# Warm-up of expert weights: the low halves of six experts computed on VectorE instead of GpSimd, and one GELU moved ahead

## The chip, the cores and the metric

The kernel runs on one core of a Trainium2 chip. The metric is the time of one execution on the device, in microseconds (us). Engines are named as the profile names them: PE is TensorE (PEld its weight loads), DVE is VectorE, ACT is ScalarE, POOL is GpSimd, SP is SyncE, which here issues all transfers.

## The reference

Sixteen batches of 256 tokens with 256 features pass through four sublayers, each with a residual. Layer norms stand in front.

```python
x = x + latent_cross_attention(ctx, layernorm(x))     # 8 heads of 128, keys from ctx and x: 512 of them
x = x + ffn_with_token_updates(layernorm(x))          # 256 -> 1024, exact GELU, -> 256
x = x + cross_attention(layernorm(x), ctx, ctx)       # one head of 256
x = x + experts(layernorm(x))                         # 8 experts, all computed, weighted by a router

# experts:
gate = einsum('btd,edi->beti', x, Wg)                 # (8, 256, 256) weights per expert
up = einsum('btd,edi->beti', x, Wu)
h = silu(gate) * up
out = einsum('bte,betd->btd', weights, einsum('beti,eid->betd', h, Wd))
```

## The kernel before, in words

**Three products for one.** Every operand of a large product is split into a high half (the value rounded to fp32r by a copy) and a low half (value minus high half). `product` issues three matmuls for each part: high by high, high by low, low by high. The high halves are made by ACT (names ending in `_high`), the low halves by DVE (`_low`), with a subtraction that has to follow its high. Expert weights are split once, in three pieces each (gate, up and down: `expert_piece`), and stay in memory.

**Two programs one behind the other.** `latent_attention` is the first sublayer: a loop over 16 batches with 8 heads, slots h = 0 to 7. In a slot PE computes the scores of head h + 1 into two `sim` banks, then works through an order of fills (K, Q, V projections, transposed probabilities T, outputs O) in a ring of four PSUM banks. A fill waits until the low half of the fill four places ahead of it has been taken out of the same bank (`ring_lo`). ACT takes the high half and computes the exponentials, DVE the low half and the maxima, POOL normalises the probabilities. `ffn_attention_experts` holds the other three sublayers. Its first batch is worked in beside the last batch of the first program, by hooks: `beside(h, done)` is called at named places in each engine's order of that batch. Where a hook stands in the order of its own engine decides what it is ahead of, since each engine works strictly through its own list.

**The turns.** After that, `rest()` runs turns t = 1 to 16. Turn t carries the chain of batch t (feed-forward, attention) and the experts of batch i = t - 1, interleaved: PE does gate e, up e, a piece of the chain, down e - 1. Between experts ACT does `silu` and `hidden_high`, DVE `hidden`, `hidden_low` and `weigh` (expert e's weighted sum), with the steps of the chain between. Turn 1 is written out by itself (`warm`): in it the weights of experts 2 to 7 are also split. PE's `split(e)` makes it wait for `warm_lo` to reach 3e + 3 ahead of gate e. Turns 2 to 14 are a hardware loop, 15 and 16 follow. All other turns have no splitting in them.

**The places that the change touches.** In turn 1, ACT does the highs of the experts at places that `WARM_AT` lists: expert 2 at the head of the turn, expert 3 between the second and the third GELU, experts 4 and 5 behind hidden_high 2, expert 6 behind the V copy, expert 7 behind hidden_high 4. POOL does all their lows (`expert_low`, L1042 to L1046), in the order 2, 3, 4, 5, then an rstd, 6, an rstd, 7. Experts 0 and 1 are split by ACT and DVE earlier. In the last batch of the first program, `gelu_high(0, 3)` and `gelu_low(0, 3)` stand behind K 4 of slot 2 on ACT and on DVE; h_fill(0, 3), which they read, stands behind K 4 on PE.

Of the kernel before, what the change touches and what calls it, by code (L numbers as in the profile page):

```python
# [9 lines left out]
ALU = mybir.AluOpType  # L10
# [11 lines left out]
def f32(ap):  # L22

    return ap.bitcast(F32)
# [723 lines left out]
def ffn_attention_experts(nc, ctx, mem, first, x1, ctxT, out, W1T, b1, W2T, b2, scale, WqT, bq, WkT, bk, WvT, bv, Wg, Wu,  # L748
# [9 lines left out]
    HC = HID // P  # L758
# [48 lines left out]
    Q, K, V, PT = 0, 2, 4, 6  # L807
# [97 lines left out]
    def expert_piece(e, j):  # L905
        return [w[e][:, j].rearrange("p c d -> p (c d)") for w in (we_raw, weh, wel)]

    WARM_AT = {2: 0, 3: 1, 4: 2, 5: 2, 6: 3, 7: 4}

    def warm_in(slot):  # L910

        return [e for e, s in WARM_AT.items() if s == slot]

# [90 lines left out]
    def gpsimd(pool):  # L1004
        def take(s, value):

            pool.wait_ge(s, value)
            pool.sem_inc(took, 1)

        def rstd_of(n, w):  # L1010
            take(var_ready[w], n + 1)
            nc.gpsimd.tensor_scalar(veps[:], mv[:, :, 1], EPS, 1.0, ALU.add, ALU.mult).then_inc(veps_ready[w], 1)
            pool.wait_ge(veps_ready[w], n + 1)
            nc.gpsimd.tensor_tensor(rstd[:], veps[:], mhalf[:], ALU.pow).then_inc(rstd_ready[w], 1)

        def bias_x1(n):

            pool.wait_ge(ln_ready["A"], n + 1)
            nc.gpsimd.tensor_tensor(x1_s[:], x1_s[:], b2_b[:].unsqueeze(1).to_broadcast([P, ST, D]), ALU.add)\
                .then_inc(x1_biased, 1)  # L1020

        def bias_x2(n):

            pool.wait_ge(ln_ready["B"], n + 1)
            nc.gpsimd.tensor_tensor(x2_s[:], x2_s[:], bv_b[:].unsqueeze(1).to_broadcast([P, ST, D]),
                                    ALU.add).then_inc(x2_biased, 1)

        def odd_rows(n):

            take(lo["A"], n + 1)  # L1030
            for part, xt in enumerate((xth, xtl)):
                nc.gpsimd.tensor_copy(
                    od[:, :, 0:8 * NL].rearrange("p c (i z h) -> p c i z h", i=NL, h=2)[:, :, :, :, part],
                    f32(xt[:, :, 2:2 + 2 * NL:2]).unsqueeze(3).to_broadcast([P, DC, NL, NL]))
            for xt, w2 in ((xth, w2h), (xtl, w2l)):
                for half in range(2):
                    last = nc.gpsimd.tensor_copy(
                        behind(w2, half),
                        f32(xt[:, half, 2 + 2 * NL:2 + 4 * NL:2]).unsqueeze(1).to_broadcast([P, NL, NL]))
            last.then_inc(od_ready, 1)  # L1040

        def expert_low(e):  # L1042
            for j in range(3):
                pool.wait_ge(warm_hi, 3 * e + j + 1)
                raw, dh, dl = expert_piece(e, j)
                nc.gpsimd.tensor_tensor(dl, raw, f32(dh), ALU.subtract).then_inc(warm_lo, 1)  # L1046

        def early(h):
            if h == 0:
                for zero in (w2_gaps(w2h), w2_gaps(w2l)):  # L1050
                    last = nc.gpsimd.memset(f32(zero), 0.0)
                last.then_inc(consts, 1)
            if h == 4:
                for zero in (od[:], up1[:], up2[:], gr[:]):
                    last = nc.gpsimd.memset(f32(zero), 0.0)
                for e in range(E):
                    last = nc.gpsimd.memset(index[:, e:e + 1], float(e))
                last.then_inc(consts, 1)
                pool.wait_ge(consts, 2)
                pool.wait_ge(small_in, 16 * 8)  # L1060

        def beside(h, done):
            if (h, done) == (0, "begin"):
                rstd_of(0, "A")
            if (h, done) == (0, "probs"):
                pool.wait_ge(w12_lo, 4)
                odd_rows(0)
                bias_x1(0)
            if (h, done) == (4, "begin"):
                rstd_of(0, "B")  # L1070
            if (h, done) == (4, "probs"):
                bias_x2(0)
                rstd_of(1, "A")
            if (h, done) == (5, "probs"):
                bias_x1(1)
            if (h, done) == (7, "probs"):
                odd_rows(1)
                rstd_of(0, "C")

        def rest():  # L1080
            def turn(t, chain, more, warm):
                if warm:
                    pool.wait_ge(warm_lo, 6)
                    for e in (2, 3, 4, 5):
                        expert_low(e)
                if chain:
                    rstd_of(t, "B")
                    bias_x2(t)
                if warm:
                    expert_low(6)  # L1090
                if more:
                    rstd_of(t + 1, "A")
                    bias_x1(t + 1)
                if warm:
                    expert_low(7)
                if more:
                    odd_rows(t + 1)
                if chain:
                    rstd_of(t, "C")
            sections_of(pool, turn)  # L1100
        return Beside(early, beside, rest)

    def scalar(act):
# [10 lines left out]
        def expert_high(e, j):  # L1114
            act.wait_ge(expert_in[e], 3 * 16)
            raw, high, _ = expert_piece(e, j)
            nc.scalar.activation(high, raw, ACT.Copy).then_inc(warm_hi, 1)
# [65 lines left out]
        def softmax_exps(t):  # L1183

            act.wait_ge(max_ready, t + 1)
            cd = halves(bank(t, "S"))
            for k in range(ST):
                last = nc.scalar.activation(pr[:, k, :], cd[:, k, :], ACT.Exp, bias=nmax[:, k:k + 1],
                                            accum_out=rsum[:, k:k + 1])
            last.then_inc(hi["S"], 1)  # L1190
# [23 lines left out]
        def beside(h, done):  # L1214
# [9 lines left out]
                gelu_high(0, 1)  # L1224
            if (h, done) == (1, ("T", 1, 1)):
                gelu_high(0, 2)
            if (h, done) == (2, ("K", 4)):
                gelu_high(0, 3)
            if (h, done) == (2, ("T", 2, 1)):
                context_high(0)  # L1230
# [36 lines left out]
        def rest():  # L1267
            def turn(t, chain, more, warm):
                i = t - 1

                for e in warm_in(0) if warm else ():
                    for j in range(3):
                        expert_high(e, j)
                silu(i, 1)
                routing_exps(i)
                hidden_high(i, 1)
                if chain:
                    gelu_high(t, 0)
                    gelu_high(t, 1)
                for e in warm_in(1) if warm else ():  # L1280
                    for j in range(3):
                        expert_high(e, j)
                if chain:
                    gelu_high(t, 2)
                    gelu_high(t, 3)

                silu(i, 2)
                if chain:
                    context_high(t)
                hidden_high(i, 2)  # L1290
                for e in warm_in(2) if warm else ():
                    for j in range(3):
                        expert_high(e, j)
                if chain:
# [6 lines left out]
                if chain:  # L1301
                    biased_high(t, "K", K, bk_s)
                    copy_high(t, "V", hh[:, V:V + 2, :])
                for e in warm_in(3) if warm else ():
                    for j in range(3):
                        expert_high(e, j)

# [1 line left out]
                if chain:  # L1309
                    copy_high(t, "B", xth[:])  # L1310
                hidden_high(i, 4)
                for e in warm_in(4) if warm else ():
                    for j in range(3):
                        expert_high(e, j)
                if chain:
# [5 lines left out]
                hidden_high(i, 5)  # L1321
                if chain:
                    softmax_exps(t)

                silu(i, 6)
                if chain:
                    copy_high(t, "T", hh[:, PT:PT + 2, :])
                if more:
                    copy_high(t + 1, "A", xth[:])
                hidden_high(i, 6)  # L1330

                silu(i, 7)
                hidden_high(i, 7)
# [11 lines left out]
    def vector(dve):  # L1345
# [231 lines left out]
        def beside(h, done):  # L1577
# [14 lines left out]
                gelu_low(0, 1)  # L1592
            if (h, done) == (1, ("T", 1, 1)):
                gelu_low(0, 2)
            if (h, done) == (2, ("K", 4)):
                gelu_low(0, 3)
            if (h, done) == (2, ("T", 2, 1)):
                context_low(0)
# [50 lines left out]
        def rest():  # L1649
            def turn(t, chain, more, warm):  # L1650
# [5 lines left out]
                for n in range(HC // 2):  # L1656
                    if chain:
                        gelu_low(t, n)
                    if n + 1 < 4:
                        routing(i, n + 1)  # L1660
                weigh(i, 0)

                hidden(i, 2)
                if chain:
                    context_low(t)
                hidden_low(i, 2)
                if chain:
                    for k in range(ST):
                        g_low(t, k)
# [7 lines left out]
                if chain:  # L1677
                    biased_low(t, "K", K, bk_s)
                    norm_apply(t, "B", x2_s)
                    copy_low(t, "V", hl[:, V:V + 2, :], hh[:, V:V + 2, :])  # L1680
                weigh(i, 2)

                if more:
# [5 lines left out]
                if more:  # L1689
                    norm_apply(t + 1, "A", x1_s)  # L1690
                hidden_low(i, 4)
                weigh(i, 3)
                if chain:
                    biased_low(t, "Q", Q, bq_s)
# [7 lines left out]
                if chain:  # L1702
                    inverses(t)
                weigh(i, 4)

                hidden(i, 6)
                if chain:
# [2 lines left out]
                    copy_low(t + 1, "A", xtl[:], xth[:])  # L1710
                hidden_low(i, 6)
                weigh(i, 5)
                if chain:
                    third_residual(t)
                    norm_stats(t, "C", x2_s)
# [408 lines left out]
```

## Time and profile before

| what | value |
|---|---|
| median of three runs | 2024.44 us (2023.81 to 2024.59) |
| the profiled execution's own time | 2024.44 us |
| its span, first to last instruction | 2022.4 us |
| PE busy, share of the span | 1973.4 us, 98% |
| DVE busy | 1380.0 us, 68% |
| ACT busy | 1107.5 us, 55% |
| POOL busy | 386.0 us, 19% |
| mean granted PE clock | 0.997 of full speed |

The busy share says which engine is nearest to having no room. A timeline has one row for an instruction or several alike; a note in square brackets gives how long its engine sat idle ahead of it and which instruction released it. PE's matmuls are drawn overlapping, so start times are the safe thing to compare.

### The profile page before, as it was taken

Reading aid. Unit: us, or ns where it says so; the run is one execution under the profiler, and the core shown is the slowest. Engines: PE = TensorE matmul, PEld = TensorE weight load, DVE = VectorE, ACT = ScalarE, POOL = GpSimd, SP = SyncE. Lnnn points to the kernel's source line nnn. Section 1 sums busy time; section 2 is a strip of 40 time slices with the busy share of each in tenths; the row PEclk is TensorE's granted clock in tenths of the full one; section 3 lists DMA queues with packets and bytes.
Section 4 is the critical chain, followed back from the end, with each engine's and each line's share of the span. In section 5 each row is a group of like instructions: output and inputs, shape, how many; then the busy total and the mean of one; then the engine's idle time right before and its main releaser. Section 6 shows DMA issues by size and latency. Waiting matters only on the chain.

```text
span 2022.4 us, 41689 instructions
## 1 busy us (share of the span) xinstructions
PE 1973.4 (98%) x14272; PEld 1855.1 (92%) x14272; DVE 1380.0 (68%) x3402; ACT 1107.5 (55%) x2285; POOL 386.0 (19%) x631
## 2 busy tenths in 40 slices
PE   7999999999999999999988999999999999999998
PEld 6889888888888888898877999999999999999998
DVE  7876767767767667767756666667666666766655
ACT  5655556555655556555555654555445555554552
POOL 2222222222222222222212511011111110111100
PEclk9999999999999999999999999999999999999999
DMA  4000000000000000000014000000000000000000
GB/s 159 12 22 21 10 10 21 21 21 10 10 21 21 18 3 21 21 21 10 6 38 137 12 18 17 17 11 11 17 11 16 16 17 11 17 11 17 11 6 11
DMA packets 47210, 44.51 MB, mean 22 GB/s; under 512 B 6848, under 2 KB 45376, under 8 KB 47168
## 3 DMA queue, kind: packets, MB, share of 16 engines
q1 hardware_dynamic: 47168, 43.96, 6.9%
q8 instruction: 25, 0.41, 0.1%
q14 instruction: 17, 0.14, 0.0%
HBM read 34.77 MB, written 8.39 MB: 21 GB/s over the span
## 4 chain that ended last, share of the span: by engine, by line
PE 86%; ACT 5%; DVE 5%; issue 2%; SPq 1%; POOL 1%; DMA 0%; ACTq 0%; DVEq 0%; POOLq 0%
PE ring L615 9%; PE ring L617 9%; PE ring L616 9%; PE ring L1741 8%; PE ring L1743 8%; PE ring L1742 8%; PE ring L668 4%; PE sim L1743 3%; PE sim L1741 3%; PE sim L1742 3%; PE sim L615 3%; PE sim L617 2%; PE sim L616 2%; PE ps_x L1741 2%; PE ps_x L1743 2%
## 5 line engine op out<-in xcount | busy, mean ns | idle before, releaser
L1741 PE MATMUL ring<-b_xch,b_weh 128*128 128x256 f32 x1024 | 293.7, 287 | 3.0 <-DVE b_act_e L1396 1.6
L1742 PE MATMUL ring<-b_xcl,b_weh 128*128 128x256 f32 x1024 | 289.7, 283 | 0.0
L1743 PE MATMUL ring<-b_xch,b_wel 128*128 128x256 f32 x1024 | 289.7, 283 | 0.0
L408 ACT ACTIVATE a_pr<-sim,a_nmax 128x512 f32<-128x512 f32 x256 | 174.3, 689 | 206.2 <-DVE a_nmax L534 206.1
L323 POOL TENSOR_SCALAR a_pr<-a_pr,a_rinv 128x512 f32<-128x512 f32 x256 | 182.9, 728 | 500.8 <-DVE a_rinv L544 498.0
L1741 PEld LDWEIGHTS ring<-b_xch,b_weh 128*128 128x128 f32 x1024 | 196.4, 192 | 3.4 <-DVE b_act_e L1396 1.8
L1742 PEld LDWEIGHTS ring<-b_xcl,b_weh 128*128 128x128 f32 x1024 | 196.5, 192 | 0.0
L1743 PEld LDWEIGHTS ring<-b_xch,b_wel 128*128 128x128 f32 x1024 | 196.4, 192 | 0.0
L1396 DVE TENSOR_TENSOR b_act_e<-b_act_e,ring 128x512 f32<-128x512 f32 x128 | 88.0, 688 | 132.9 <-PE ring L1743 130.9
L525 DVE TENSOR_TENSOR a_ptl<-ring,a_pth 128x512 fp32r<-128x512 f32 x256 | 163.7, 680 | 3.4 <-ACT a_pth L398 2.3
L512 DVE SCALAR_TENSOR_TENSOR a_ktl<-ring,a_bkv_s,a_kth 128x512 fp32r<-128x512 f32 x128 | 95.3, 744 | 102.0 <-ACT a_kth L388 102.0
L534 DVE TENSOR_REDUCE a_nmax<-sim 128x1 f32<-128x512 f32 x256 | 163.4, 679 | 1.1 <-PE sim L617 1.1
L1126 ACT ACTIVATE b_act_e<-ring 128x512 f32<-128x512 f32 x128 | 76.4, 597 | 159.0 <-PE ring L1743 158.7
L1130 ACT ACTIVATE b_heh<-b_act_e 128x512 fp32r<-128x512 f32 x128 | 80.9, 632 | 140.7 <-DVE b_act_e L1396 140.7
L615 PE MATMUL ring<-a_pth,a_vh 128*128 128x256 f32 x512 | 146.0, 285 | 3.7 <-DVE a_ptl L525 3.7
L521 DVE TENSOR_TENSOR a_vl<-ring,a_vh 128x512 fp32r<-128x512 f32 x128 | 88.5, 691 | 84.4 <-ACT a_vh L396 84.3
L616 PE MATMUL ring<-a_ptl,a_vh 128*128 128x256 f32 x512 | 145.9, 285 | 0.0
L617 PE MATMUL ring<-a_pth,a_vl 128*128 128x256 f32 x512 | 145.8, 285 | 0.0
L398 ACT ACTIVATE a_pth<-ring 128x512 fp32r<-128x512 f32 x256 | 139.7, 603 | 3.9 <-PE ring L668 3.8
L396 ACT ACTIVATE a_vh<-ring 128x512 fp32r<-128x512 f32 x128 | 76.6, 599 | 110.8 <-PE ring L617 110.8
L668 PE MATMUL ring<-ident,a_pr 128*128 128x128 f32 x1024 | 133.3, 273 | 1.2 <-DVE a_ktl L512 0.9
L668 PEld LDWEIGHTS ring<-ident,a_pr 128*128 128x128 f32 x1024 | 117.9, 140 | 14.5 <-DVE a_ktl L512 1.4
(356 smaller groups left out, 6332.8 us busy)
## 6 DMA issues: line engine op xcount, KB each, us to landing
a_c_in<-in_ctx_in SPq DMA_DIRECT2D x16, 256.0 KB, 2.7
a_x_in<-in_x SPq DMA_DIRECT2D x16, 256.0 KB, 2.9
a_x_res<-in_x SPq DMA_DIRECT2D x16, 256.0 KB, 2.7
x_between<-a_x_out SPq DMA_DIRECT2D x16, 256.0 KB, 2.2
b_x_s<-x_between SPq DMA_DIRECT2D x16, 256.0 KB, 2.6
b_up<-b_ev SPq DMA_DIRECT2D x256, 1.0 KB
out_x<-b_acc SPq DMA_DIRECT2D x16, 256.0 KB, 2.2
b_ct_raw<-in_ctxT SPq DMA_DIRECT2D x15, 256.0 KB, 2.6
```

Of the source, the lines that this page charges most:

```text
L323: nc.gpsimd.tensor_scalar(pr[:, h % 2, t, :], pr[:, h % 2, t, :], rinv[:, h % 2, t:t + 1], 1.0, ALU.mult, ALU.mult).then_inc(prob_ready, 1)
L398: nc.scalar.activation(pth[:, :, name[2] * P:(name[2] + 1) * P], bank[:].rearrange("p (k q) -> p k q", k=KT), ACT.Copy).then_inc(ring_hi, 1)
L408: nc.scalar.activation(pr[:, h % 2, t, :], sim[t][:], ACT.Exp, bias=nmax[:, h % 2, t:t + 1], accum_out=rsum[:, h % 2, t:t + 1]).then_inc(e ...
L525: nc.vector.tensor_tensor(ptl[:, :, cols], bank[:].rearrange("p (k q) -> p k q", k=KT), f32(pth[:, :, cols]), ALU.subtract).then_inc(ring_ ...
L534: nc.vector.tensor_reduce(nmax[:, h % 2, t:t + 1], sim[t][:], AX.X, ALU.max, negate=True)\
L615: nc.tensor.matmul(out, lh, rh, start=(n == 0), stop=False)
L616: nc.tensor.matmul(out, lh, rl, start=False, stop=False)
L617: last = nc.tensor.matmul(out, ll, rh, start=False, stop=(n == len(parts) - 1))
L668: last = nc.tensor.transpose(bank[:, k * P:(k + 1) * P], pr[:, h % 2, t, k * P:(k + 1) * P], ident[:])
L1741: nc.tensor.matmul(out, lh, rh, start=(n == 0), stop=False)
L1742: nc.tensor.matmul(out, lh, rl, start=False, stop=False)
L1743: last = nc.tensor.matmul(out, ll, rh, start=False, stop=(n == len(parts) - 1 and not more))
```

## The change

Six things are edited, and no work is added or left out.

- DVE does the lows of experts 2 to 7 in turn 1, at six places of its order; POOL does none.
- ACT does their highs at six other places, one expert at each.
- The four GELUs of turn 1 follow each other on ACT with nothing between.
- The places are: expert 2 behind the GELUs (DVE: behind weigh 0), expert 3 behind hidden_high 2 (hidden_low 2), expert 4 behind the V copy (V low), expert 5 behind hidden_high 4 (hidden_low 4), expert 6 behind the softmax exponentials (weigh 4), expert 7 behind hidden_high 6 (weigh 5).
- In the last batch of the first program, `gelu_high(0, 3)` and `gelu_low(0, 3)` go from behind K 4 to the beginning of slot 2, ahead of the exponentials (ACT) and the maxima (DVE) of head 3.
- POOL's turn keeps only its rstd values, the bias additions and `odd_rows`.

```diff
-    WARM_AT = {2: 0, 3: 1, 4: 2, 5: 2, 6: 3, 7: 4}
+    WARM_AT = {2: 0, 3: 1, 4: 2, 5: 3, 6: 4, 7: 5}
...
-        def expert_low(e):
-            for j in range(3):
-                pool.wait_ge(warm_hi, 3 * e + j + 1)
-                raw, dh, dl = expert_piece(e, j)
-                nc.gpsimd.tensor_tensor(dl, raw, f32(dh), ALU.subtract).then_inc(warm_lo, 1)
...
-                if warm:
-                    pool.wait_ge(warm_lo, 6)
-                    for e in (2, 3, 4, 5):
-                        expert_low(e)
...
-            if (h, done) == (2, ("K", 4)):
+            if (h, done) == (2, "begin"):
                 gelu_high(0, 3)
...
                 silu(i, 1)
                 routing_exps(i)
                 hidden_high(i, 1)
+                if chain:
+                    for n in range(HC // 2):
+                        gelu_high(t, n)
                 for e in warm_in(0) if warm else ():
                     for j in range(3):
                         expert_high(e, j)
...
-            if (h, done) == (2, ("K", 4)):
+            if (h, done) == (2, "begin"):
                 gelu_low(0, 3)
...
                 weigh(i, 0)
+                for e in warm_in(0) if warm else ():
+                    for j in range(3):
+                        expert_low(e, j)
...
                 hidden_low(i, 2)
+                for e in warm_in(1) if warm else ():
+                    for j in range(3):
+                        expert_low(e, j)
...
                     copy_low(t, "V", hl[:, V:V + 2, :], hh[:, V:V + 2, :])
+                for e in warm_in(2) if warm else ():
+                    for j in range(3):
+                        expert_low(e, j)
                 weigh(i, 2)
...
                 hidden_low(i, 4)
+                for e in warm_in(3) if warm else ():
+                    for j in range(3):
+                        expert_low(e, j)
                 weigh(i, 3)
...
                 weigh(i, 4)
+                for e in warm_in(4) if warm else ():
+                    for j in range(3):
+                        expert_low(e, j)
...
                 weigh(i, 5)
+                for e in warm_in(5) if warm else ():
+                    for j in range(3):
+                        expert_low(e, j)
```

The function that DVE calls exists already:

```python
        def expert_low(e, j):
            dve.wait_ge(warm_hi, 3 * e + j + 1)
            raw, dh, dl = expert_piece(e, j)
            nc.vector.tensor_tensor(dl, raw, f32(dh), ALU.subtract).then_inc(warm_lo, 1)
```

## Rows read from the trace of the kernel before

**Rows 1.** The page's first part: busy us (share of the span), instructions
```profile
PE 1973.4 (98%) x14272; PEld 1855.1 (92%) x14272; DVE 1380.0 (68%) x3402; ACT 1107.5 (55%) x2285; POOL 386.0 (19%) x631
```
**Rows 2.** Timeline of PE, turn 1: start, us, instruction [idle before]: y_fill, s_fill, gate 7
```profile
1122.92 0.36 PE L1741 MATMUL sim<-b_w2h,b_hh 128*128 128x272 f32 x1 [2.75 <-DVE b_hl L1420]
...
1147.85 0.36 PE L1741 MATMUL ring<-b_hh 128*128 128x256 f32 x1 [0.52 <-DVE b_hl L1432]
...
1157.42 0.28 PE L1741 MATMUL ring<-b_xch,b_weh 128*128 128x256 f32 x1
```
**Rows 3.** Timeline of PE, turn 2: gate 2, y_fill, gates 4, 5, 6, 7
```profile
1179.05 0.28 PE L1741 MATMUL ring<-b_xch,b_weh 128*128 128x256 f32 x1
...
1181.93 0.29 PE L1741 MATMUL sim<-b_w2h,b_hh 128*128 128x272 f32 x1
...
1197.02 0.28 PE L1741 MATMUL ring<-b_xch,b_weh 128*128 128x256 f32 x1
...
1203.22 0.28 PE L1741 MATMUL ring<-b_xch,b_weh 128*128 128x256 f32 x1
...
1208.98 0.28 PE L1741 MATMUL ring<-b_xch,b_weh 128*128 128x256 f32 x1
...
1215.60 0.28 PE L1741 MATMUL ring<-b_xch,b_weh 128*128 128x256 f32 x1
```
**Rows 4.** Timeline of DVE, turn 2: weigh 0, hidden_low 2, V, hidden_low 4, weigh 4, 5
```profile
1180.93 0.87 DVE L1413 SCALAR_TENSOR_TENSOR b_acc<-ring,b_wts,b_x_s 128x256 f32<-128x256 f32 x2
...
1183.59 0.69 DVE L1400 TENSOR_TENSOR b_hel<-b_act_e,b_heh 128x512 fp32r<-128x512 f32 x1
...
1197.39 0.69 DVE L1426 TENSOR_TENSOR b_hl<-ps_c,b_hh 128x512 fp32r<-128x512 f32 x1
...
1201.99 0.69 DVE L1400 TENSOR_TENSOR b_hel<-b_act_e,b_heh 128x512 fp32r<-128x512 f32 x1
...
1210.17 0.87 DVE L1413 SCALAR_TENSOR_TENSOR b_acc<-ring,b_wts,b_acc 128x256 f32<-128x256 f32 x2
...
1214.93 0.87 DVE L1413 SCALAR_TENSOR_TENSOR b_acc<-ps_x,b_wts,b_acc 128x256 f32<-128x256 f32 x2
```
**Rows 5.** By tile and line (ns min/median/max, first and last start); DVE's timeline, expert 1
```profile
L1046 POOL TENSOR_TENSOR b_wel<-b_wel_raw,b_weh x18: 1278/1292/1317, 1107.8 to 1149.7; 128x512 fp32r<-128x512 f32 x18
...
L1505 DVE TENSOR_SCALAR b_near<-b_sig x16: 165/167/1284, 1107.9 to 1985.7; 128x16 f32<-128x16 f32 x16
...
L1117 ACT ACTIVATE b_weh<-b_wel_raw x24: 614/617/632, 1089.9 to 1144.0; 128x512 fp32r<-128x512 f32 x24
...
1102.21 1.88 DVE L1385 TENSOR_TENSOR b_wel<-b_wel_raw,b_weh 128x512 fp32r<-128x512 f32 x3
```
**Rows 6.** Timelines of PE, ACT and DVE beside slots 1 and 2, last batch
```profile
1039.24 0.28 PE L1769 MATMUL ps_x<-b_zm,b_up 128*128 128x256 f32 x1
...
1042.23 1.04 PE L668 MATMUL ring<-ident,a_pr 128*128 128x128 f32 x8
1043.76 0.36 PE L1741 MATMUL ps_c<-b_w2h,b_hh 128*128 128x272 f32 x1 [0.49 <-DVE b_hl L1420]
...
1035.18 0.84 ACT L1140 ACTIVATE b_gel<-ps_c,b_b_s 128x256 f32<-128x256 f32 x2 [0.70 <-PE ps_c L1769]
...
1038.05 0.69 ACT L408 ACTIVATE a_pr<-sim,a_nmax 128x512 f32<-128x512 f32 x1
...
1037.33 1.28 DVE L534 TENSOR_REDUCE a_nmax<-sim 128x1 f32<-128x512 f32 x2
1040.11 0.75 DVE L512 SCALAR_TENSOR_TENSOR a_ktl<-ring,a_bkv_s,a_kth 128x512 fp32r<-128x512 f32 x1 [1.50 <-ACT a_kth L388]
```
**Rows 7.** PE's timeline, slot 7; slices: busy PE, PEld, DVE, ACT, POOL, PEclk, DMA, GB/s
```profile
1083.91 0.55 PE L615 MATMUL ring<-a_pth,a_vh 128*128 128x256 f32 x1 [2.26 <-DVE a_ptl L525]
...
1084.00:1085.00 1.00, 1.00 (x5) 1.00 (x6) 0.36 (x1) 0.00 (x0) 0.47 (x4) 0.50 0.10 18
...
1087.00:1088.00 1.00, 1.00 (x10) 1.00 (x9) 0.48 (x1) 0.32 (x1) 0.00 (x0) 0.88 0.01 2
```

More of the change, by code:

```diff
@@ L1088, in turn @@
                     bias_x2(t)
-                if warm:
-                    expert_low(6)
                 if more:
@@ L1093, in turn @@
                     bias_x1(t + 1)
-                if warm:
-                    expert_low(7)
-                if more:
                     odd_rows(t + 1)
@@ L1269, in turn @@
                 i = t - 1
-                for e in warm_in(0) if warm else ():
-                    for j in range(3):
-                        expert_high(e, j)
                 silu(i, 1)
@@ L1277, in turn @@
                 if chain:
-                    gelu_high(t, 0)
-                    gelu_high(t, 1)
-                for e in warm_in(1) if warm else ():
+                    for n in range(HC // 2):
+                        gelu_high(t, n)
+                for e in warm_in(0) if warm else ():
                     for j in range(3):
                         expert_high(e, j)
-                if chain:
-                    gelu_high(t, 2)
-                    gelu_high(t, 3)
                 silu(i, 2)
@@ L1290, in turn @@
                 hidden_high(i, 2)
-                for e in warm_in(2) if warm else ():
+                for e in warm_in(1) if warm else ():
                     for j in range(3):
@@ L1303, in turn @@
                     copy_high(t, "V", hh[:, V:V + 2, :])
-                for e in warm_in(3) if warm else ():
+                for e in warm_in(2) if warm else ():
                     for j in range(3):
@@ L1311, in turn @@
                 hidden_high(i, 4)
-                for e in warm_in(4) if warm else ():
+                for e in warm_in(3) if warm else ():
                     for j in range(3):
@@ L1323, in turn @@
                     softmax_exps(t)
+                for e in warm_in(4) if warm else ():
+                    for j in range(3):
+                        expert_high(e, j)
                 silu(i, 6)
@@ L1330, in turn @@
                 hidden_high(i, 6)
+                for e in warm_in(5) if warm else ():
+                    for j in range(3):
+                        expert_high(e, j)
                 silu(i, 7)
@@ L1661, in turn @@
                 weigh(i, 0)
+                for e in warm_in(0) if warm else ():
+                    for j in range(3):
+                        expert_low(e, j)
                 hidden(i, 2)
@@ L1666, in turn @@
                 hidden_low(i, 2)
+                for e in warm_in(1) if warm else ():
+                    for j in range(3):
+                        expert_low(e, j)
                 if chain:
@@ L1680, in turn @@
                     copy_low(t, "V", hl[:, V:V + 2, :], hh[:, V:V + 2, :])
+                for e in warm_in(2) if warm else ():
+                    for j in range(3):
+                        expert_low(e, j)
                 weigh(i, 2)
@@ L1691, in turn @@
                 hidden_low(i, 4)
+                for e in warm_in(3) if warm else ():
+                    for j in range(3):
+                        expert_low(e, j)
                 weigh(i, 3)
@@ L1704, in turn @@
                 weigh(i, 4)
+                for e in warm_in(4) if warm else ():
+                    for j in range(3):
+                        expert_low(e, j)
                 hidden(i, 6)
@@ L1712, in turn @@
                 weigh(i, 5)
+                for e in warm_in(5) if warm else ():
+                    for j in range(3):
+                        expert_low(e, j)
                 if chain:
```

## The prediction

> **What bounds the kernel now.** I read the page's engine line first: TensorE is busy 98% of the span and VectorE, the next, 68% [rows 1]. So an edit on another engine costs or gives time only where TensorE waits for it. Then I went through TensorE's timeline for the two stretches that the diff touches: the last batch of the first layer (about 995 to 1101 us), and the "warm" turn behind it (t = 1, about 1109 to 1171 us from h_fill to h_fill), in which experts 2 to 7 are split into a high and a low half. The reader is to see two idle notes in the warm turn: 2.75 us ahead of y_fill and 0.52 us ahead of s_fill [rows 2]. The 24 products of a gate and an up start every 0.12 us (1179.05 to 1181.93) and are drawn 0.28 us long [rows 3], so a noted wait hides 0.16 us more: they cost 2.91 and 0.68, 3.59 us together. That is all the warm turn could give back. In the first stretch the edit touches one note of 0.49 us, so 0.65 [rows 6].
>
> Last I read the second turn (t = 2, from 1171 us), which has the same order of work and no splitting. There TensorE runs through without a wait from gate 2 to gate 7 [rows 3], so it shows when VectorE would be done with each step if nothing held it [rows 4]. It is the ruler for all that follows.
>
> **Part 1: the low halves move from POOL to VectorE.** Removed from POOL: 18 subtractions of 1.292 us [rows 5], 23 us of an engine with a 19% share. Nobody waits for POOL in this turn but through these halves and the rstd values. Added to VectorE: 18 subtractions, 1.88 us for three in a row [rows 5], 11.3 us in a turn where it has room on average. But the place decides. split(e) lets gate e start only when the three lows of expert e are done, and on VectorE they now stand behind a named step of the turn just ahead of that gate. Three lows behind a step end 1.80 us after it (1.88, less the 0.08 by which neighbours overlap). Against the ruler:
>
> Expert 2, behind weigh 0: 1180.93 + 0.87 + 1.80 = 1183.60; gate 2 starts at 1179.05: 4.55 late.
> Expert 3, behind hidden_low 2: 1183.59 + 0.69 + 1.80 = 1186.08. y_fill, down 1 and g_fill lie ahead of gate 3, and y_fill alone (48 products from 1181.93) runs to about 1188: no wait.
> Expert 4, behind the V low: 1197.39 + 0.69 + 1.80 = 1199.88; gate 4 at 1197.02: 2.86 late.
> Expert 5, behind hidden_low 4: 1201.99 + 0.69 + 1.80 = 1204.48; gate 5 at 1203.22: 1.26 late.
> Expert 6, behind weigh 4: 1210.17 + 0.87 + 1.80 = 1212.84; gate 6 at 1208.98: 3.86 late.
> Expert 7, behind weigh 5: 1214.93 + 0.87 + 1.80 = 1217.60; gate 7 at 1215.60: 2.00 late [rows 3, 4].
>
> Each wait delays TensorE and with it what VectorE gets next, so the ruler starts again at each gate and the waits add: 14.53 us. What is queued behind these lows on VectorE (the next hidden, context_low, biased_low Q, third_residual) needs results of that same late gate or of fills behind it, so it finds its input late too and adds nothing.
>
> **Part 2: ScalarE's highs are regrouped.** The same 18 activations of 0.617 us [rows 5]; none is added. Expert 2's group leaves the head of the turn and expert 3's leaves the middle of the four GELUs. Then the GELUs run as in the ruler, where y_fill follows gate and up 2 at once (1179.05 to 1181.93) [rows 3]; the waits of 2.91 and, since biased_low Q keeps ahead of a late gate 5, of 0.68 go: minus 3.59. The price of the regrouping is whether highs end before VectorE wants them. Behind the last GELU copy, behind the V copy and behind the attention exponentials, three highs take 3 x 0.617 = 1.85 us at most and run while VectorE does the step named above; at worst, by my estimate, two of these groups are late by 1 us each, which is half of such a group's time. I take nothing.
>
> VectorE is also freed of something. Its 128x16 instruction of L1505 takes 167 ns in the median and 1284 ns at most, 16 times [rows 5]; the long one is in the warm turn, just after POOL began the first of its subtractions. What that delayed is in the 2.75 us already counted as gained, so it adds no term. The Trainium skill states it in SBUF — State Buffer, Who interferes with whom: a VectorE instruction in a 2-port mode, or with two inputs in SBUF while GpSimd reads SBUF, shares one port pair with GpSimd, and the loser waits for the whole instruction. By that rule the change removes a wait, and a reader who stops there forecasts a gain; the trace agrees with the rule by the 1284 against 167 ns. It is the third rival below.
>
> Warm turn: 14.53 - 3.59 = plus 10.94 us.
>
> **Part 3: gelu(0, 3) moves ahead of the exponentials of head 3.** h_fill(0, 3) is still behind K 4 on TensorE, and ends at 1039.24 + 0.28 = 1039.52 [rows 6]. ScalarE now stands waiting for it at the head of slot 2. From the start of a GELU to the start of the exponentials behind it the trace shows 1038.05 - 1035.18 = 2.87 us, GELU, copy and table load included. So they start at 1039.56 + 2.87 = 1042.43, not at 1038.05. VectorE's maxima, now behind gelu_low(0, 3), start about 1041.7 and need 0.72 us to the first exponential (1037.33 to 1038.05): 1042.42, the same. K 4's low follows the exponentials by 1040.11 - 1038.05 = 2.06: 1044.49, ending at 1045.24. Who waits: the ring has four banks, and the fills are K 4, Q 3, O 1, T(2, 0), T(2, 1). T(2, 1) takes K 4's bank. Now it runs in the row of eight transposes from 1042.23; then it starts at 1045.24, needs 0.45 us, and y_fill(0, 0) starts at 1045.7 in place of 1043.76: plus 1.93 us. Two table loads less on ScalarE and the wait of 0.49 are in this. Bounds: minus 0.65 if the fill were not held, plus 3 if the late probabilities of head 3 hold a transpose too; I take 1.93, as every step of it is a row. Nothing later takes it back: the waits that follow in this batch are all for engines that start from TensorE's own fills.
>
> **Sum.** The profiled execution took 2024.44 us with a span of 2022.4, and that is also the median of the runs. 2024.44 + 10.94 + 1.93 = 2037.3 us, 0.64% slower. Changes within 0.2% (4 us) are about what a measurement of this kernel can't tell from none.
>
> **The rivals.**
>
> Forecast (0.62): the waits stand where I put them; 2037.3. Its own range is 2033 to 2040: each of five gates may be off by some 0.6, and the highs by 2 in all.
>
> The clock falls too (0.14). After a wait of 2.26 us, behind a stretch with other waits, TensorE's granted clock stood at 0.50, the 1.2 GHz level, and came back in the slice that begins at 1087 [rows 7]; that is about 3.2 us at half speed, so 1.6 us lost. It did not fall after the 2.75 us wait of the warm turn. The new waits of 4.4 and 3.7 us are longer than that one; one to three falls cost 1.6 to 4.8: 2039 to 2042.
>
> Waits partly hidden (0.12): TensorE's delay at one gate lets VectorE and ScalarE run ahead for the next. The ruler lets them restart level; if each wait after the first were only half (4.99 of 9.98), the time is 2032.3. Speaking for it: weigh 2, the norm statistics and weigh 3 would be out of the way early. Against it: the step ahead of each group (V low, hidden_low, weigh) hangs on the newest fill, not on backlog.
>
> VectorE set free (0.07, the other side): the waits of 3.59 go, and the lows are in time. That needs all five lateness terms to sum to under 1.6 us, not 14.5; the time is 2024.44 - 3.59 + 1.93 = 2022.8, or 2020.2 if part 3 gives 0.65 as well. For it: POOL's 18 subtractions cost 1.292 each against some 0.63. Against it: POOL has them done gates ahead (neither note of the turn is theirs [rows 2]), and VectorE starts them later.
>
> About no change (0.05): half the gates wait by under 1 us, and it cancels.
>
> **How the numbers follow.** Slower by over 0.2%: forecast, clock, partly hidden, 0.88. Same 0.06, faster 0.06. The predicted time is the forecast's. The range takes in the partly hidden case below and two falls of the clock above: 2030.5 to 2041.5.
>
> **What would show it.** In the profile of the changed kernel: TensorE's first matmul of gates 2, 4, 5, 6, 7 in the warm turn each with an idle note that names VectorE's b_wel at L1385 or its neighbourhood, of about 4.4, 2.7, 1.1, 3.7 and 1.8 us (0.16 less than the cost); no note at y_fill and at s_fill; gate 7, which now starts at 1157.42 [rows 2], at about 1157.42 + 1.93 + 10.94 = 1170.3; L1505 never above 0.2 us; in the first layer's last batch a wait of about 2.4 us ahead of T(2, 1), for a_ktl, and the exponentials of head 3 near 1042.4. From the second turn on all must be as before. The prediction is wrong if VectorE's steps come before the gates by more than the ruler shows, if the lows start earlier than the step I name, or if the clock falls in more than two places.

## The result, and the profile after: 1.1% slower

The changed kernel takes 2045.77 us in the median (2044.85 to 2047.78, four runs) against 2024.12 (2023.47 to 2024.59): a ratio of 1.0108, 95% interval 1.0094 to 1.0122. I forecast slower, 2037.3 us in a range of 2030.5 to 2041.5. The direction was right and the size was not: plus 21.7 us where I had 12.9. The profiled execution took 2043.21 us with a span of 2041.4, 19.0 more than before; this execution was a quick one of its kernel (the four had 2044.85 at least), so the traces below show somewhat less than the medians' 21.7.

The page's first part for the changed kernel, busy us and share of the span, answers to [rows 1]: the work is the same and TensorE's share is one point lower.

```profile
PE 1980.0 (97%) x14272; PEld 1861.2 (91%) x14272; DVE 1387.5 (68%) x3420; ACT 1104.6 (54%) x2283; POOL 362.0 (18%) x613
```

Next, TensorE's timeline of the changed kernel: T(2, 1) in the first layer's last batch, then the first matmuls of gate 2, y_fill, gates 4 and 5, s_fill, gates 6 and 7 in turn 1. They answer to [rows 2, 6].

```profile
1043.93 0.33 PE L668 MATMUL ring<-ident,a_pr 128*128 128x128 f32 x1 [2.46 <-DVE a_ktl L512]
...
1123.19 0.58 PE L1744 MATMUL ring<-b_xch,b_weh 128*128 128x256 f32 x1 [4.45 <-DVE b_wel L1370]
...
1127.56 0.29 PE L1744 MATMUL sim<-b_w2h,b_hh 128*128 128x272 f32 x1
...
1146.24 0.38 PE L1744 MATMUL ring<-b_xch,b_weh 128*128 128x256 f32 x1 [3.43 <-DVE b_wel L1370]
...
1156.48 0.39 PE L1744 MATMUL ring<-b_xch,b_weh 128*128 128x256 f32 x1 [2.27 <-DVE b_wel L1370]
...
1160.95 0.28 PE L1744 MATMUL ring<-b_hh 128*128 128x256 f32 x1
...
1167.76 0.58 PE L1744 MATMUL ring<-b_xch,b_weh 128*128 128x256 f32 x1 [3.77 <-DVE b_wel L1370]
...
1177.84 0.39 PE L1744 MATMUL ring<-b_xch,b_weh 128*128 128x256 f32 x1 [1.89 <-DVE b_wel L1370]
```

The reader is to see that the waits stand at exactly the five gates and the one transpose that were named, that the notes at y_fill and s_fill are gone, and that three of the five have the forecast size (4.4, 3.7, 1.8) while gates 4 and 5 have 3.43 and 2.27 where 2.7 and 1.1 were forecast. Adding 0.16 to each note, the five cost 16.6 us, not 14.5.

Slices of the changed kernel, with busy time of PE, PEld, DVE, ACT and POOL, the granted clock, DMA share and GB/s, show the larger lack:

```profile
1122.00:1123.00 1.00, 0.00 (x0) 0.00 (x0) 1.00 (x2) 0.02 (x1) 0.00 (x0) 0.97 0.00 0
1123.00:1124.00 1.00, 0.81 (x3) 0.81 (x4) 0.14 (x1) 0.00 (x0) 0.00 (x0) 0.50 0.00 0
1125.00:1126.00 1.00, 1.00 (x7) 1.00 (x6) 0.00 (x0) 0.00 (x0) 0.00 (x0) 0.50 0.00 0
1126.00:1127.00 1.00, 1.00 (x9) 1.00 (x9) 0.00 (x0) 0.84 (x2) 0.00 (x0) 0.82 0.00 0
...
1147.00:1148.00 1.00, 1.00 (x6) 1.00 (x6) 0.85 (x4) 0.00 (x0) 0.00 (x0) 0.50 0.00 0
1158.00:1159.00 1.00, 1.00 (x7) 1.00 (x7) 0.00 (x0) 0.01 (x1) 0.00 (x0) 0.50 0.00 0
1169.00:1170.00 1.00, 1.00 (x6) 1.00 (x6) 0.00 (x0) 0.00 (x0) 0.00 (x0) 0.50 0.03 8
1178.00:1179.00 1.00, 1.00 (x9) 1.00 (x10) 0.97 (x4) 0.00 (x0) 0.00 (x0) 1.00 0.01 1
```

The clock falls to the 1.2 GHz level (0.50) in or behind four of the five waits (behind gate 2's wait it comes back within the slice at 1126); in this execution only the shortest, at gate 7, has no fall behind it. A whole turn, from h_fill to h_fill, in the kernel before:

```profile
1109.10:1171.01 61.91, 58.58 (x487) 58.03 (x485) 43.19 (x111) 38.71 (x73) 28.54 (x32) 1.00 0.08 26
```

and in the changed one:

```profile
1110.55:1191.53 80.98, 65.12 (x486) 63.90 (x485) 50.98 (x126) 39.70 (x75) 7.17 (x14) 0.92 0.07 20
```

19.07 us more. Waits at gates plus 16.6, notes gone minus 3.6: 13.0. The rest, 6.1 us, is the clock: its mean of 0.92 over 80.98 us means some 13 us at half speed, so about 6.5 lost by that reckoning. That is 1.5 us for each of four falls. It is one execution's price: another of the same turn, below, pays about 10 us.

Third, the lows themselves. All instructions of L1370, ns min/median/max:

```profile
L1370 DVE TENSOR_TENSOR b_wel<-b_wel_raw,b_weh x24: 658/684/1780, 1094.2 to 1177.1; 128x512 fp32r<-128x512 f32 x24
```

The groups of experts 2, 4 and 5 in VectorE's timeline:

```profile
1121.25 1.89 DVE L1370 TENSOR_TENSOR b_wel<-b_wel_raw,b_weh 128x512 fp32r<-128x512 f32 x3
...
1143.60 2.58 DVE L1370 TENSOR_TENSOR b_wel<-b_wel_raw,b_weh 128x512 fp32r<-128x512 f32 x3
...
1153.44 2.98 DVE L1370 TENSOR_TENSOR b_wel<-b_wel_raw,b_weh 128x512 fp32r<-128x512 f32 x3
```

Experts 4 and 5 take 0.7 and 1.1 us longer than expert 2, which is what their gates wait beyond the forecast. POOL's timeline at those times has one instruction running as each of these two groups starts, a bias addition:

```profile
1143.17 1.26 POOL L1025 TENSOR_TENSOR b_x_s<-b_x_s,b_bv_b 128x512 f32<-128x512 f32 x1 [0.85 <-DVE b_ln L1349]
...
1152.87 1.81 POOL L1019 TENSOR_TENSOR b_x_s<-b_x_s,b_b_b 128x512 f32<-128x512 f32 x1 [3.67 <-DVE b_ln L1349]
```

### The profile page after: what moved, and what is told of

The parts are those of the page before. It is cut to its first block, busy times and chain, and to the rows that moved or that the text cites. A ratio compares the mean times of both kernels' runs of the same rounds, so it can differ in the third digit from the quotient of the medians.

```text
span 2041.4 us, 41686 instructions
## 1 busy us (share of the span) xinstructions
PE 1980.0 (97%) x14272; PEld 1861.2 (91%) x14272; DVE 1387.5 (68%) x3420; ACT 1104.6 (54%) x2283; POOL 362.0 (18%) x613
## 4 chain that ended last, share of the span: by engine, by line
PE 87%; ACT 5%; DVE 5%; issue 2%; SPq 1%; DMA 0%; POOL 0%; ACTq 0%; DVEq 0%; POOLq 0%
PE ring L615 9%; PE ring L616 9%; PE ring L617 9%; PE ring L1744 8%; PE ring L1746 8%; PE ring L1745 8%; PE ring L668 4%; PE sim L1746 3%; PE sim L1744 3%; PE sim L1745 3%; PE sim L615 3%; PE sim L617 2%; PE sim L616 2%; PE ps_x L1744 2%; PE ps_x L1746 2%
## 5 line engine op out<-in xcount | busy, mean ns | idle before, releaser
L1744 PE MATMUL ring<-b_xch,b_weh 128*128 128x256 f32 x1024 | 296.9, 290 | 18.8 <-DVE b_wel L1370 15.8
```

The costliest lines, as they stand in the source:

```text
L1744: nc.tensor.matmul(out, lh, rh, start=(n == 0), stop=False)
```

## The experiments

The kernel before ran beside each on the same chip, at 2024.1 to 2024.3 us in the median.

**Part 3 alone.**

```diff
-            if (h, done) == (2, ("K", 4)):
+            if (h, done) == (2, "begin"):
                 gelu_high(0, 3)          # and gelu_low(0, 3) on DVE
```

> The kernel before with part 3 alone: gelu(0, 3) at the beginning of slot 2 on ScalarE and VectorE. My theory: T(2, 1) waits about 2.4 us for K 4's low, plus 1.9 us; the clock then falls for y_fill and takes about 1.5 more: 2026 to 2028 us. Rival, the edit is hidden behind other fills and saves two table loads: 2023.5 to 2024.5 us.

2027.55 us, ratio 1.0018 (1.0008 to 1.0028). Its list of TensorE's waits (total, times, longest) has the new one:

```profile
PE ring L668 <- DVE a_ktl L512: 2.5, 1, 2.5
```

and its slices the clock behind it:

```profile
1046.00:1047.00 1.00, 1.00 (x6) 1.00 (x5) 1.00 (x3) 0.80 (x2) 0.57 (x1) 0.50 0.00 0
```

As my theory had it: plus 3.3 us over the 2024.20 beside it, some 2 from the wait and the rest in the size of one fall. The rival is out.

**The warm turn alone.** The changed kernel with the two hooks of part 3 put back to `("K", 4)`.

> The changed kernel with part 3 undone, so the edits of the warm turn alone. My theory, waits at gates 2, 4, 5, 6, 7 of 16 us together and clock falls behind most of them, about 1.5 us each: 2041 to 2045 us. Rival, the waits do not come from the warm turn's lows but the delay is handed on from the first stretch: under 2036 us.

2043.20 us (2039.09 to 2045.15). The warm turn makes 19.0 of the 21.7 us, and the two parts add within the spread of 6 us that this kernel shows: 19.0 + 3.3 = 22.3. Its turn from h_fill to h_fill, and two slices of it, behind gates 2 and 7:

```profile
1108.61:1193.45 84.84, 69.10 (x487) 67.89 (x486) 50.96 (x126) 39.74 (x75) 7.20 (x14) 0.86 0.06 20
...
1125.00:1126.00 1.00, 1.00 (x7) 1.00 (x6) 0.00 (x0) 0.34 (x1) 0.00 (x0) 0.50 0.00 0
...
1179.00:1180.00 1.00, 1.00 (x7) 1.00 (x6) 0.83 (x3) 0.00 (x0) 0.00 (x0) 0.50 0.01 2
```

The instructions are those of the changed kernel's turn and the five notes are as long in sum (15.7 us, 15.8 there), yet the turn took 84.84 us where the changed kernel's took 80.98. The clock makes the difference. It fell behind all five waits, gate 7's 1.90 us too, and behind gates 2 and 4 it stayed down for about 6 us with TensorE busy, not for 3 to 3.5. With 16.5 us of waits, the clock's part is here 10.0 us, against 6.1.

**TensorE kept busy in the waits.** Same kernel, and ahead of each split:

```diff
+            def busy(e, times, i, warm):
+                if warm:
+                    pe.wait_ge(silu_done, i * E + e)
+                    for _ in range(times):
+                        into(ps_g, 0, e - 1)
...
+                busy(2, 3, i, warm)      # 4: 2 times, 5: 1, 6: 3, 7: 1
                 split(2)
                 gate(i, 2)
```

This adds 120 matmuls, whose results are overwritten.

> As the run with the warm turn's edits alone, but TensorE is kept busy in the waits: ahead of each split(e) it computes gate e - 1 again into the gate bank (3, 2, 1, 3 and 1 times, 12 matmuls of 0.12 us each), results that the true gate e overwrites. Theory that the clock's falls are what my sum lacked: the waits for the lows end at the same instants after their gates, no slice below 1.00 in the turn, and some 5 to 6 us less than without the refill: about 2036 to 2039 us. Rival, the falls cost nothing apart and the waits were mis-sized: the same as without, 2041 to 2045 us, or more, as the added matmuls are late themselves.

2035.19 us (2034.72 to 2036.26), 0.8 below the range that I expected: 120 more matmuls make the kernel 8.0 us faster than the one without. Busy time over the warm turn (1104 to 1184 here) and the clock:

```profile
1104.00:1184.00 80.00, 77.94 (x643) 76.92 (x643) 53.19 (x134) 41.76 (x78) 7.23 (x14) 1.00 0.11 34
```

The same stretch without the refill:

```profile
1104.00:1186.00 82.00, 66.26 (x463) 65.05 (x462) 48.44 (x121) 39.22 (x74) 7.20 (x14) 0.85 0.10 33
```

The gates start as late as ever: gate 2 at 1120.95, 4.6 us after down 0 gives TensorE free (1116.36). The whole turn takes 75.59 us: 58.3 without any wait (61.91 less 3.6), 16.6 of waits, and 0.7 left over. So the gain is the clock's, and this shows the larger of the two terms that I lacked. It lies between the 6.1 us read from the changed kernel's profile and the 10.0 of the profiled execution without the refill.

**The lows back on POOL, in the new order.** ScalarE as in the changed kernel; POOL does 2, 3, rstd B, 4, rstd A, 5, 6, odd rows, 7.

```diff
-                for e in warm_in(0) if warm else ():
-                    for j in range(3):
-                        expert_low(e, j)           # on DVE, six such places
+                if warm:
+                    pool.wait_ge(warm_lo, 6)
+                    expert_low(2)                  # on POOL, and so on
+                    expert_low(3)
```

> The warm turn's new places on ScalarE, but the lows on POOL as before the change (order 2, 3, rstd B, 4, rstd A, 5, 6, odd rows, 7). Theory that the late places of the highs are the cause and the engine only adds: each group ends one high plus 3.84 us after its place, later than VectorE's by 0.5 to 1.6 us; 2045 to 2052 us, above the run with VectorE's lows. Rival, VectorE's queue is the cause: the waits go with the lows, 2022 to 2030 us.

2055.86 us (2053.76 to 2057.85), above its own range of 2045 to 2052. Its waits, total, times and longest:

```profile
PE ring L1744 <- POOL b_wel L1046: 23.8, 5, 5.3
```

Going back to POOL does not take the waits away; it makes them 8 us longer in sum than VectorE's 15.7, and the clock falls behind all five. So VectorE's queue is not the cause. That the late place is, the early lows below show.

**POOL's bias additions out of the way.** The warm turn alone, and:

```diff
                     rstd_of(t, "B")
+                    if warm:
+                        pool.wait_ge(warm_lo, 15)
                     bias_x2(t)               # bias_x1 likewise, at 18
```

> The warm turn's edits alone, with one more: in that turn POOL's bias additions wait until expert 4's and expert 5's lows are done on VectorE, so the two engines never read SBUF at once there. Theory, the shared port stretches the lows at gates 4 and 5 (2.58 and 2.98 us for three in place of 1.88): these notes shrink from 3.4 and 2.3 to about 2.7 and 1.1 us, three lows last 1.9 us everywhere, and the time falls by about 2 us, or 3 with a shorter clock fall: 2040 to 2042 us. Rival, the lows are late for their highs: notes unchanged, 2043 us.

2038.81 us (2038.69 to 2040.11), 4.4 less than without. TensorE's first matmul of gate 4:

```profile
1143.28 0.58 PE L1748 MATMUL ring<-b_xch,b_weh 128*128 128x256 f32 x1 [2.73 <-DVE b_wel L1374]
```

VectorE's lows of all experts, ns min/median/max:

```profile
L1374 DVE TENSOR_TENSOR b_wel<-b_wel_raw,b_weh x24: 656/683/686, 1089.1 to 1171.5; 128x512 fp32r<-128x512 f32 x24
```

and the sum of TensorE's waits for them, with their number and the longest:

```profile
PE ring L1748 <- DVE b_wel L1374: 14.0, 5, 4.4
```

The longest low is 686 ns, not 1780, gate 4's note is 2.73 us as first forecast, and the sum of the five fell from 15.7 to 14.0. So the second term, 1.7 us, is shown to come from POOL's additions running beside the lows; that the two share a port is the reading of it. The remaining 2.7 us of the gain lies in the clock. The turn's last column but two says how much of it was at half speed:

```profile
1106.95:1187.32 80.37, 66.38 (x487) 65.26 (x485) 49.16 (x126) 39.65 (x75) 6.68 (x14) 0.89 0.06 19
```

There are four falls in it, none behind gate 5, whose note is now 1.17 us, where the run without this edit has five. But the falls in one and the same turn differ between executions by more (6.1 against 10.0 us above), so these 2.7 us can't be laid to the edit.

**The whole change with both causes taken out.** The bias additions late, TensorE refilled 3, 2, 3 and 1 times ahead of experts 2, 4, 6 and 7, part 3 in place.

> The whole change with both of the causes that my sum lacked taken out of the warm turn: POOL's bias additions wait for the lows of experts 4 and 5, and TensorE computes gate e - 1 again (3, 2, 3 and 1 times ahead of experts 2, 4, 6 and 7) in the waits. Part 3 stays, with its clock fall. Theory that the forecast's terms were right and these two were missing: notes and refill together as forecast, about 2036 to 2038 us. Rival, a further cause: above 2040 us, or below 2034 us.

2037.14 us (2036.79 to 2037.96), against my forecast of 2037.3 for the change itself. With the two lacking terms removed, its other terms add up to what is measured. The agreement to 0.2 us is partly luck: part 3's own fall of about 1.5 us is in it, and so is a gain of 1.5 us in the later turns, below; and the turn itself took 73.80 us, 0.95 over the forecast 61.91 + 10.94.

**Earlier highs, lows on POOL.** From the kernel before:

```diff
-    WARM_AT = {2: 0, 3: 1, 4: 2, 5: 2, 6: 3, 7: 4}
+    WARM_AT = {3: 1, 4: 2, 5: 2, 6: 3, 7: 4}
...
-                for j in range(3):
-                    expert_high(1, j)
+                for e in (1, 2):
+                    for j in range(3):
+                        expert_high(e, j)
                 silu(0, 0)
...
                 if chain:
                     gelu_high(t, 2)
                     gelu_high(t, 3)
+                for e in warm_in(1) if warm else ():     # was between GELU 1 and 2
+                    for j in range(3):
+                        expert_high(e, j)
```

> The kernel before with only ScalarE's highs moved: expert 2's into ScalarE's wait for gate 0, expert 3's behind the four GELUs; the lows stay on POOL. Theory: y_fill's wait comes from the GELU chain behind these highs and from POOL's port hold on VectorE's routing steps; its note of 2.75 us goes, s_fill's stays: about 2021.3 us (2020.5 to 2022.5). Rival, POOL's lows of expert 2 now hold up VectorE ahead of gate 1, or gate 3 waits: 2024 us or more.

2020.75 us (2019.66 to 2021.34), ratio 0.9982 (0.9972 to 0.9992). The first line is s_fill's note, which stays; the second is y_fill's, which was 2.75 us:

```profile
PE ring L1739 <- DVE b_hl L1430: 0.5, 1, 0.5
...
PE sim L1739 <- DVE b_hl L1418: 0.2, 1, 0.2
```

The larger part of what part 2 was credited with can be had without moving a single low: the turn takes 59.34 us in place of 61.91. Where the last 0.9 of the 3.5 us comes from is not shown; the profiled execution was 0.9 us ahead already at 979 us, long before the edited places.

**Early lows on VectorE.** The same highs, those of experts 4 and 5 spread about the two g_highs, and the lows on VectorE at other places:

```diff
+                for e in (1, 2):                 # ahead of hidden(0, 0)
+                    for j in range(3):
+                        expert_low(e, j)
...
                 hidden_low(i, 2)                 # + expert 3
                 g_low(t, 0)                      # + expert 4
                 weigh(i, 1)                      # + expert 5
...
                 biased_low(t, "Q", Q, bq_s)      # + expert 6
...
                 weigh(i, 4)                      # + expert 7
```

> All lows on VectorE as in the changed kernel, but each group about one gate earlier, in idle time of the second turn's timeline: expert 2 behind expert 1, 3 behind hidden_low 2, 4 behind the first g_low, 5 behind weigh 1, 6 behind biased_low Q, 7 behind weigh 4; highs early enough for each. Theory, the place and not the engine costs the time: no note names b_wel, y_fill's and s_fill's notes go too, h_fill to h_fill about 58.6 us: 2020 to 2021.5 us. Rival, VectorE has no room for 18 more: waits of 1 us or more at gates with clock falls behind them, above 2026 us.

2017.76 us (2016.89 to 2018.67), ratio 0.9971 (0.9959 to 0.9982), the fastest kernel here: 6.5 us under before and 28 under the change, with the same 18 subtractions on the same engine. The turn from h_fill to h_fill:

```profile
1106.57:1165.29 58.72, 58.38 (x486) 57.97 (x485) 46.98 (x123) 38.06 (x72) 7.22 (x14) 1.00 0.09 27
```

No wait in it names b_wel. The one new note is of 0.3 us ahead of o_fill, whose input, the low half of T, now stands behind expert 7's lows on VectorE. The traces account for 4.7 of the 6.5 us: 3.2 in this turn (61.91 less 58.72) and 1.5 in the later turns. The rest lies ahead of the edited places, where executions differ: the profiled one was 2.2 us ahead of the kernel before at 979 us, and that of the same kernel run again was level with it there.

**How much code POOL holds.** Kernels with the lows on POOL show 13 short waits in the later turns that the others don't (last section). So to the kernel with early lows I added 18 memsets of one column on POOL at the head of turn 1, that nobody waits for, and ran that kernel without them again:

```diff
+                for n in range(18 if warm else 0):
+                    nc.gpsimd.memset(pad[:, n:n + 1], 0.0)
                 if chain:
                     rstd_of(t, "B")
```

> The early lows on VectorE, with 18 memsets of one column each on POOL in turn 1, which nobody waits for. All kernels with 18 lows in POOL's turn 1 show 13 notes of 2.4 us together ahead of the transposes of the third norm in the later turns; those without show none. Theory that this hangs on how much code POOL's turn 1 holds: the notes come back and the time rises by 1 to 1.5 us, to about 2019 us. Rival, it hangs on another engine's order or on timing: no notes, 2017.5 to 2018 us.

> The early lows on VectorE once more, beside the run with POOL's memsets: 2017 to 2018.5 us, no note ahead of the transposes of the third norm.

2018.76 (2017.24 to 2019.74) and 2017.98 us (2017.07 to 2019.65), with no such notes in either; the two times do not stand apart. The theory fell; see the last section.

## Why the prediction was off, point by point

**Where the waits stand: right.** Five gates, T(2, 1), none at expert 3, and both old notes gone.

**The sum of part 1: too low by 2.1 us.** The terms were 4.55, 2.86, 1.26, 3.86, 2.00; measured, with 0.16 added to each note, 4.61, 3.59, 2.43, 3.93, 2.05. The second turn is a ruler good to 0.07 us for three of them. The step that failed for the other two is "three lows behind a step end 1.80 us after it": it holds only while no addition of POOL runs beside them. I had the port rule in hand, with 1284 against 167 ns, and used it in one direction alone, as something VectorE is freed of. VectorE was indeed freed at L1505 (its longest is now 169 ns), but POOL still has two additions in this turn, and the subtractions that moved have two inputs in SBUF. The rule (the Trainium skill, SBUF — State Buffer, Who interferes with whom) puts exactly such an instruction against a GpSimd one that reads SBUF; the trace agrees by 2.58 and 2.98 against 1.88 us, and the run with the additions moved shows it.

**Part 2, minus 3.59: right.** Both notes went, here and in the early variants.

**Part 3, plus 1.93: right as a wait.** From the end of h_fill(0, 3) to the exponentials it took 1041.06 - 1038.16 = 2.90 us where I had 2.91, and the note is 2.46 us for some 2.4.

**The clock: the step that failed.** I made it a rival with a chance of 0.14, though two of my own waits, 4.4 and 3.7 us, were longer than any that the warm turn had before, and my one counterexample was a single wait of 2.75 us. It was no alternative to the waits but a consequence of them: behind waits of 4.45, 3.43, 2.27, 3.77 and 2.46 us the clock fell each time, at about 1.5 us each in this execution, the size that I had priced (1.6). One to three falls was my count; it was four in the turn and one in part 3, and five in the turn, two of them near 3 us, in the run with the warm turn alone. Since the cause was made a separate case, its price stood in neither the point nor, in full, the range.

**The balance** for the profiled executions (plus 19.0 us of span): forecast 12.9; clock in the warm turn 6.1; longer waits 2.1; the stretch ahead of the turn came out 0.5 below its 1.93; the later turns minus 1.5. That makes 19.1. The 0.5 is an accident of two executions: the changed kernel's was 1.0 us ahead already at a note near 979 us, before any edited place (978.35 against 979.35). From there its stretch took 2.45 us more, part 3's wait with falls of the clock at 1044 and 1068 us in place of one at 1084, and less a note of 0.46 us at 1073.91 that went and that the sum did not have.

**The other rivals.** Partly hidden waits: no, each gate waited as if the others had not. VectorE set free: the relief is real but of no use while lows come late.

## What to carry to other kernels

When work moves to an engine with room, ask not whether it fits in the turn but what it stands behind and how long ahead of its consumer; the same subtractions on the same engine cost 19 us in one order and gave 6 in another, 4.7 of which the traces show where they arise. A turn of the same loop without the extra work is a ruler for that, good to a tenth of a microsecond. Where such a wait is forecast on TensorE, price the clock's fall behind it in the forecast itself: of the six new waits here five, of 2.3 to 4.5 us, had one. Price it as a range: the same turn paid 6.1 us in one execution and 10.0 in another.

## What was not expected of the hardware

Added matmuls made the kernel faster: 120 of them, 8.0 us less. The length of a wait does not decide alone whether the clock falls: in the kernel before, 2.75 us ahead of y_fill passed without a fall and 2.26 us in slot 7 did not [rows 2, 7]; in the changed kernel the same 2.26 us in slot 7 did pass, and 2.27 us at gate 5 did not. Nor does the kernel decide it: of two executions of the kernel with early lows, one had a fall behind the 2.26 us of slot 7, at 1084 us, and the other none there but one at 1091, behind a wait of 1.87 us.

From the second turn on, kernels with the lows on POOL (before, part 3 alone, lows back on POOL, early highs) show 13 waits ahead of the third norm's transposes, 2.4 us together, while those without show none though none of them runs other instructions in those turns. From the second turn's h_fill to the end the changed kernel and the early lows take 849.9 and 849.8 us, the kernel before and the early highs 851.4 both. Eighteen memsets on POOL that nobody waits for in turn 1 did not bring the waits back. Why they come is open.
